# Folding the values of batches 1 to 3 head by head from 64 rows, in a gated attention and feed-forward kernel with a new prologue order

## The reference, cut to what matters

```python
q = layernorm(x) @ Wq; k = ctx @ Wk; v = ctx @ Wv          # per head
o = softmax(q @ k.T / 8) @ v                               # 77 keys
x = x + tanh(g_xattn) * (o @ Wo + bo)
n = layernorm(x)
g = act_quant(n) @ weight_quant(w_gate).T                  # 512 -> 2048
u = act_quant(n) @ weight_quant(w_up).T
h = square(relu(g)) * u
x = x + tanh(g_ffn) * (act_quant(h) @ weight_quant(w_down).T)
```

## Time and profile before

| | us |
|---|---|
| median of 3 runs | 1192.84 |
| the profiled execution, its own time | 1192.0 |
| its span | 1190.1 |
| PE busy | 1169.0 |
| DVE busy | 1035.5 |
| ACT busy | 869.1 |
| POOL busy | 307.0 |

### The profile page before, as it was taken

How to read it: one execution, slowest core, us unless ns; L and a number is a source line. 1 busy time by engine, 2 the same in 40 slices (tenths; PEclk the granted TensorE clock), 3 DMA queues, 4 the chain that set the end, 5 groups by cost and what they waited for, 6 DMA issues and landing times.

```text
span 1190.1 us, 18790 instructions
## 1 busy us (share of the span) xinstructions
PE 1169.0 (98%) x5802; PEld 742.8 (62%) x5867; DVE 1035.5 (87%) x2124; ACT 869.1 (73%) x929; POOL 307.0 (26%) x313
## 2 busy tenths in 40 slices
PE   9989899999999999999999999999999999999998
PEld 7656556666665666666566656656665666666554
DVE  4989898888988888888998888888899888988887
ACT  4877777776886777677877767776787777677764
POOL 3222222222442222222442222222244222222200
PEclk9999999999999999999999999999999999999999
DMA  9792654443444464444444464443443444444333
GB/s 354 263 302 67 156 142 109 98 108 93 101 115 102 114 167 110 97 103 107 101 99 98 114 178 112 98 107 94 101 114 97 104 97 110 96 99 112 84 65 75
DMA packets 286484, 144.69 MB, mean 122 GB/s; under 512 B 254586, under 2 KB 255226, under 8 KB 283889
## 3 DMA queue, kind: packets, MB, share of 16 engines
q1 hardware_dynamic: 286445, 144.32, 47.4%
q10 hardware_dynamic: 4, 0.00, 0.0%
HBM read 57.86 MB, written 24.35 MB: 69 GB/s over the span
## 4 chain that ended last, share of the span: by engine, by line
PE 88%; DVE 4%; DMA 3%; ACT 3%; issue 2%; SPq 0%; POOL 0%; ACTq 0%; DVEq 0%; POOLq 0%
PE gu_ps L1084 34%; PE o_ps L1048 18%; PE y_ps L1098 17%; PE s_ps L66 17%; DMA v_scr<-x 1%; DMA w_down<-in_wu_t 1%; DVE staged L1324 1%; PE gu_ps L1148 1%; DVE half_max L1330 1%; DMA a_scr<-a_spare 1%; DVE w_down L1484 0%; ACT staged L730 0%; ACT x L762 0%; PE y_ps L1141 0%; ACT k_pairs L864 0%
## 5 line engine op out<-in xcount | busy, mean ns | idle before, releaser
L1084 PE MATMUL gu_ps<-w_up,xq_t 128*128 128x512 bf16 x1024 | 241.9, 379 | 0.7 <-DVE staged L1324 0.7
L1084 PE MATMUL gu_ps<-w_gate,xq_t 128*128 128x512 bf16 x951 | 226.3, 379 | 8.6 <-DMA xq_t<-xq 3.9
L1098 PE MATMUL y_ps<-w_down,hq_t 128*128 128x512 bf16 x1008 | 227.8, 379 | 0.0
L1048 PE MATMUL o_ps<-v_sb,pt_high 128*128 128x512 f32 (+1 forms) x640 | 212.8, 413 | 1.1 <-DVE pt_low L1313 1.1
L1324 DVE TENSOR_TENSOR staged<-staged,gu_ps 128x1024 f32<-128x1024 f32 x128 | 155.6, 1215 | 53.8 <-ACT staged L784 53.8
L66 PE MATMUL s_ps<-a_sb,xf_high 128*128 128x308 f32 x1024 | 187.3, 305 | 0.0
L1084 PEld LDWEIGHTS gu_ps<-w_up,xq_t 128*128 128x128 bf16 x1024 | 99.5, 98 | 122.8 <-DVE staged L1324 2.6
L645 POOL TENSOR_TENSOR rstd<-var_eps,neg_half 128x1 f32<-128x1 f32 x128 | 96.6, 755 | 307.9 <-DVE var_eps L1289 275.2
L824 ACT ACTIVATE staged<-staged,h_scale 128x1024 f32<-128x1024 f32 x126 | 137.9, 1141 | 48.7 <-DVE h_scale L1344 48.7
L1098 PEld LDWEIGHTS y_ps<-w_down,hq_t 128*128 128x128 bf16 x1008 | 97.8, 97 | 119.7
L778 ACT ACTIVATE staged<-gu_ps 128x1024 f32<-128x1024 f32 x127 | 128.9, 1015 | 53.9 <-PE gu_ps L1084 53.5
(11 more groups left out here) (146 smaller groups left out, 1439.7 us busy)
## 6 DMA issues: line engine op xcount, KB each, us to landing
xf_sb<-in_x_feat SPq DMA_DIRECT2D x64, 256.0 KB, 2.7
x_sb<-in_x_tok SPq DMA_DIRECT2D x64, 256.0 KB, 2.8
y<-staged SPq DMA_DIRECT2D x63, 256.0 KB, 2.0
staged<-in_wg_t SPq DMA_DIRECT2D x4, 1024.0 KB, 9.8
staged<-in_wd_t SPq DMA_DIRECT2D x4, 1024.0 KB, 7.5
folded<-a_scr SPq DMA_DIRECT2D x3, 1232.0 KB, 5.3
v_scr<-x SPq DMA_DIRECT2D x12, 256.0 KB
folded<-v_scr SPq DMA_DIRECT2D x3, 1024.0 KB, 5.0
```

The source lines that it names most:

```text
L1048: last = nc.tensor.matmul(o_ps[:, :], pt[0:rows, P * c:P * (c + 1)], v_sb[0:rows, v, c, :], start=(c == 0 and pt is pt_high and v == 0), s ...
L1084: last = nc.tensor.matmul(target[:, q, :], xq_t[:, s.par(0), c, :], w[:, c, cols], start=(c == 0), stop=(c == DC - 1))
L1098: last = nc.tensor.matmul(y_ps[:, :], hq_t[:, c, :], w_down[:, c, :], start=(c == 0), stop=(c == FC - 1))
```

## The change

- Batch 0 keeps the fold by pairs of heads. For batches 1 to 3 the values of one head lie side by side (231 keys), and are folded in two halves of 116 and 115 keys by one matmul each that contracts the 64 rows of that head, taken right out of `v_t` at row 0 or row 64 (`tile_position`). That makes 16 matmuls with 16 copies (`take_later_values(k)`) in place of 24 matmuls with 15 copies. `place_values` stays for batch 0 alone.
- Each half lies over two batches, so it is stored by two DMAs, 32 in place of 15. The DRAM scratch is row by row, and `load_values` reads it in rows of 2 KB where it read 8 KB for each partition.
- Piece 0 of w_down is loaded into `v_pairs`, once the fold of batch 0 has read it, and no longer waits for a slot of `staged`. The first `relu_half` waits for the up piece in slot 0 and no longer for down piece 0.
- The prologue lists of all engines are new. SP issues all eight pieces of gate and up without a wait among them, ahead of the first key store; x of tile 0 comes ahead of the others, x_feat of tile 1 and x of tiles 1 to 3 behind the first key store, x_feat of tile 3 nearly last. DVE measures 5 pieces (4 before) and scales 6 (7 before); ACT measures 7 (8 before) and scales 6 counting the two of the first step (5 before).
- In the first step DVE's `top_half(0)` stands behind `shift_scores(3)`. The second step has a list of its own: `hidden_half(1)` right behind `unmark_input`, `probs_low` of the third tile within it, `sum_probs` last.

```diff
+FIRST_ROWS = ((BATCH - 1) * KEYS + 1) // 2
+V_LATER = 2 * HEADS
...
+def head_part(k):
+    h, s = divmod(k, 2)
+    return h, KEYS + FIRST_ROWS * s, FIRST_ROWS - s
...
         def raw(m, p):
+            if m == 2 and p == 0:
+                return v_pairs[:, :, :].rearrange("p q n -> p (q n)")[:, 0:PIECE]
...
                 def load_down(p):
-                    sp.wait_ge(weight_stage[1][UP_SLOT.index(p)], DONE)
+                    if p == 0:
+                        sp.wait_ge(vo_done, KC)
+                    else:
+                        sp.wait_ge(weight_stage[1][UP_SLOT.index(p)], DONE)
...
+                def store_later_values(k):
+                    at = KEYS * head_part(k)[0]
+                    sp.wait_ge(vo_taken, k + 1)
+                    for b, j, n, r in part_runs(k):
+                        sp.dma_start(v_scr[b, at + j:at + j + n, :],
+                                     v_slots[k % V_OUT_RING][r:r + n, :]).then_inc(v_stored[k % V_OUT_RING], 16)
...
+                def take_later_values(k):
+                    rows = head_part(k)[2]
+                    act.wait_ge(vo_done, KC + k + 1)
+                    if k >= V_OUT_RING:
+                        act.wait_ge(v_stored[k % V_OUT_RING], 32 * (k // V_OUT_RING))
...
+                def fold_later_values(k):
+                    h, first, rows = head_part(k)
+                    if k < V_RING:
+                        pe.wait_ge(v_split_done, KC + k - V_RING + 1)
+                    else:
+                        pe.wait_ge(vo_taken, k - V_RING + 1)
+                    own = slice(HEAD * (h % 2), HEAD * (h % 2 + 1))
+                    nc.tensor.matmul(value_slots[(KC + k) % V_RING][0:rows, :], v_t[own, h // 2, first:first + rows], wo_sb[own, h // 2, :],
+                                     start=True, stop=True, tile_position=(HEAD * (h % 2), 0)).then_inc(vo_done, 1)
...
# SP, the loads ahead of the first key store (after)
+                load_x(start, 0)
                 load_weight(1, 2, wu_t)
+                load_weight(0, 1, wg_t)
+                load_weight(1, 3, wu_t)
+                load_weight(0, 2, wg_t)
+                load_weight(0, 3, wg_t)
+                load_weight(1, 0, wu_t)
+                load_weight(1, 1, wu_t)
+                store_keys(1, 0)
...
# DVE, from the first measured piece of the new list (after)
+                measure(1, 3)
+                first_values_low(0)
+                measure(0, 2)
+                first_values_low(1)
+                top_scores(start, 0)
+                shift_scores(start, 0)
+                sum_rows(0)
+                measure(1, 0)
+                find_unit(0)
+                scale(0, 0)
+                sum_probs(start, 0)
...
+                scale(2, 0)
+                sum_probs(start, 2)
+                scale(2, 1)
+                ternary(2, 1, w_down)
+                probs_low(start, 1)
+                ternary(2, 0, w_down)
...
+                def second_step(s):
+                    unmark_hidden(s, -1)
+                    hidden_half(s, 0)
+                    add_attention(s, 1)
+                    input_scale(s, 1)
+                    top_scores(s, 3)
+                    unmark_input(s, 1)
+                    hidden_half(s, 1)
+                    shift_scores(s, 3)
+                    input_stats(s, 3)
+                    top_half(s, 0)
+                    probs_low(s, 2)
+                    hidden_unit_scale(s, 1)
+                    top_half(s, 1)
+                    hidden_scales(s)
+                    sum_probs(s, 3)
```

More of the change, by code:

```diff
@@ L955, in _ @@
                 gate_bias()
-                high_part(start, 1)
                 first_keys(2)
@@ L968, in _ @@
+                take_later_values(0)
+                scale(0, 2)
                 take_keys(1, 2)
-                first_values(3)
-                measure(1, 3)
+                take_later_values(1)
+                high_part(start, 1)
                 take_keys(1, 3)
-                first_values(4)
+                take_later_values(2)
+                take_later_values(3)
+                take_keys(2, 0)
+                take_later_values(4)
                 probs_high(start, 0)
-                take_keys(2, 0)
@@ new lines, in _ @@
+                take_later_values(7)
+                mark_input(start, 0)
+                measure(2, 1)
+                take_later_values(8)
+                exponentials(start, 1)
+                take_later_values(9)
+                take_keys(3, 0)
+                take_later_values(10)
+                measure(2, 3)
+                part_probs(start, 1)
+                take_keys(3, 1)
+                take_later_values(11)
+                take_later_values(12)
+                take_keys(3, 2)
@@ L1533, in first_step @@
                     hidden_half(s, 0)
-                    top_half(s, 0)
                     add_attention(s, 1)
@@ L1552, in step @@
                         return
-                    if s.has(1) and not s.opens(1) and s.has(3):
+                    if s.opens(1):
+                        second_step(s)
+                        return
+                    if s.has(1) and not s.opens(2) and s.has(3):
                         probs_low(s, 1)
@@ L1559, in step @@
                         finish(s, -2)
-                    if s.has(3) and not s.opens(1):
+                    if s.has(3):
                         input_stats(s, 3)
@@ L1621, in _ @@
-                split_bias()
-                dve.wait_ge(tanh_done, 1)
-                first_values_low(0)
-                measure(0, 3)
-                first_values_low(1)
-                sum_probs(start, 0)
-                sum_rows(0)
-                first_values_low(2)
+                ternary(0, 0, w_gate)
+                sum_rows(1)
+                scale(0, 1)
+                ternary(0, 2, w_gate)
+                ternary(0, 1, w_gate)
+                find_unit(1)
+                find_hidden_unit()
@@ L1629, in _ @@
+                probs_low(start, 0)
+                scale(1, 2)
+                scale(1, 0)
+                ternary(1, 3, w_up)
+                ternary(1, 0, w_up)
+                add_attention(start, 0)
+                input_scale(start, 0)
+                ternary(1, 1, w_up)
+                top_scores(start, 1)
+                shift_scores(start, 1)
+                unmark_input(start, 0)
+                ternary(1, 2, w_up)
+                sum_probs(start, 1)
                 dve.wait_ge(rstd1_done, 2)
@@ L1645, in _ @@
[L1645 to L1656 removed]
+                measure(2, 2)
                 top_scores(start, 2)
@@ L1668, in _ @@
                 ternary(2, 0, w_down)
-                probs_low(start, 1)
-                ternary(2, 1, w_down)
                 steps(dve, step, (-2, -1, 0, 1, 2, 3, 4))
```

316 lines of the change are left out of this document (128 added, 188 removed).

## The result

The changed kernel takes **1201.98 us** (median of 4 runs, 1201.02 to 1202.95), the kernel before 1193.20 beside it (4 runs, 1191.83 to 1194.35): a ratio of 1.0078, 95% interval 1.0063 to 1.0093. It is about 9 us slower, where 1189.3 was forecast and 1184.3 to 1196.0 given as range. The profiled execution has a span of 1199.2 us.

The account below looks back on a forecast made before the run. Steady steps go at PE's pace, so the start of gate_up(3, 0), paced by DVE and ACT, decides. The walk gave -2.6 us with crowded durations, -4.6 with usual ones; taken -3.5: 1192.84 - 3.5 = 1189.3 us, range 1184.3 to 1196.0.

Parts of the forecast that it names:

- The value stores: Prologue, values of batches 1 to 3: a round trip is two issues (0.9 us), a landing (4.25 to 6.94) and a copy (0.6).
- The slower rival: Prologue: value slots' round trips make the last take late, at 92.5 us, giving 1198 us; chance 0.18.
- the ring of three value slots: Value parts share three slots: five round trips where four sufficed, 8.0 us left for each; from about 9.2 the sign turns.
- PE's work: Prologue folds: eight fewer at 0.86 us each are 6.9 us less, lying beside DVE's work.
- the bound below: PE's folds: if neighbours in different row halves ran together, 4 x 0.86 = 3.4 us less.
- the prediction's bound above: PE's folds: 0.19 us for each of 16 if its weight load is no longer covered, 3 us more.
- Loads: Prologue: pieces land from 24.4 to 38.5 us; DVE's first measure starts 1.3 us later, row sums no longer wait 2.3 us.
- DVE's list: Prologue: 58.8 us of work from 27.2, waits under 0.3 us, first step at 86.0, 4.5 us ahead.
- ACT's end of the prologue: Join at 79.7 us against 82.31, relu at 85.5 against 88.13; gate_up(0, 0) starts at 82, not 85.42.
- the walk of the first step: ACT from relu to the mark of tile 1: 8.1 us, mark at 93.6 against 97.57, so -4.0 us.
- Second step: 3.4 us of PE waits removed, but later sum_probs delays the mark 2.7 us; some 2.4 us come back at tile 3.
- The reload in 2 KB rows: Reload of values lies beside the step's other work: nothing counted; if it showed, three reloads below 1 us each.

Follow-up runs that it names:

- e17: Changed kernel with x_feat of tile 3 loaded early, old second step, DVE's first_values_low(2) early and parts of 109 and 122 rows: 1190.31 us, ratio 0.9994.
- e16: Kernel before with each value store cut in two, 38 and 90 rows (52 and 52 of the last chunk): 1197.23 us, ratio 1.0037.
- e15: Kernel before with each value store cut in two, 64 and 64 rows (52 and 52 of the last chunk): 1192.12 us, ratio 0.9995.
- e4: Kernel before with the folds by heads alone (16 parts, 32 stores, 2 KB reload), prologue order and first two steps as before: 1198.34 us, ratio 1.0046.
- e14: Kernel before with the folds by heads alone, parts cut at 109 and 122 rows instead of 116 and 115: 1193.50 us, ratio 1.0016.
- e13: Changed kernel with the parts of a head cut at 109 and 122 rows instead of 116 and 115: 1198.83 us, ratio 1.0057.
- e9: Kernel before with the folds by heads alone, one store a part (18 stores instead of 32), rows in another order: 1206.63 us, ratio 1.0119.
- e18: Kernel before with the folds by heads alone, 18 stores, 112 rows a part, some rows left out: 1194.38 us, ratio 1.0023.
- e11: Kernel before with one fold matmul for each value chunk of batches 1 to 3 (15 in place of 24): 1193.40 us, ratio 1.0012.
- e5: Changed kernel with small unused matmuls (14, 7, 5 and 14) added at four places where PE waited: 1201.99 us, ratio 1.0058.
- e7: Changed kernel with x_feat of tile 3 early, DVE's old second step and small unused matmuls (14, 8, 4, 9) in PE's waits: 1196.53 us, ratio 1.0027.
- e2: Changed kernel with DVE's second step in the order of before: 1197.87 us, ratio 1.0040.
- e3: Changed kernel with x_feat of tile 3 loaded early and DVE's second step in the order of before: 1197.08 us, ratio 1.0036.
- e1: Changed kernel with x_feat of tile 3 loaded right behind the last down piece: 1200.97 us, ratio 1.0059.
- e8: Kernel before with the folds by heads alone, every odd part folded twice (24 matmuls, as many as before): 1200.25 us, ratio 1.0068.
- e6: Kernel before with the folds by heads alone, small unused matmuls added ahead of part 8 (16) and gate_up(1, 0) (14): 1198.74 us, ratio 1.0065.

## Why the prediction was wrong, point by point

The forecast was -3.5 us and the result is +9. Two terms have runs that size them in the changed kernel: the second step (+1 of gain forecast, 4 us of loss measured) and the value stores (nothing forecast beyond their round trip, about 3 us measured, with intervals that overlap). The late x_feat adds 1. With x_feat early, the old second step, no 38-row stores and DVE's low part early (e17) the time is level with before or below it.

**The value stores** (the step that failed first). The prediction priced a part's store as "two issues (0.9 us), a landing (4.25 to 6.94 us) and a copy", and let the down pieces land in the time of before. It never asked what 77, 39 and 38 rows do where 128 and 104 stood. What the runs showed: with the number of stores and the bytes the same, the rows of a store alone change the time, and 38 rows are bad. In the kernel before this costs 5.1 us (e16 over e15), in the head folds 4.8 (e4 over e14; intervals just overlap), in the changed kernel 3.1 (over e13; they overlap), and 116 and 115 rows cost 12.3 (e9 over e18). The Trainium skill states the rule ("DMA: Bandwidth & Descriptors", Why a DMA increments its semaphore by 16 and not by 1): a transfer that SP or ACT issues runs on the largest number of engines up to 16 that divides its outermost dimension, the lowest-numbered ones. By that rule 38 rows run on 2 engines, 116 on 4, 115 on 5, 112, 64 and 128 on 16. An estimate worked out from this rule, rows of 2 KB on the fullest engine over all value stores, stands in the table. The times of the kernels with pair folds (before, e15, e16) rise with it, and so do those with head folds, but for e18 and e14, whose intervals overlap. So the times agree with the rule; no view here shows single engines, so that these are the ones the page names is not shown.

| kernel | rows of its stores | rows on the fullest engine, by the page | us |
|---|---|---|---|
| e18 | 112, 56 | 117 | 1194.4 |
| before | 128, 104 | 120 | 1192.4 to 1192.9 |
| e15 | 64, 52 | 120 | 1192.1 |
| e14 | 77, 32, 45 | 152 | 1193.5 |
| e4 | 77, 39, 38 | 288 | 1198.3 |
| e16 | 38, 90, 52 | 324 | 1197.2 |
| e9 | 116, 115 (77, 39, 38 in two parts) | 400 | 1206.6 |

**The slower rival** (1198 us, chance 0.18) got the sign and the queue right and 5 of the 9 us, and the mechanism wrong: what it got right is luck. It was to be the ring of three value slots, with ACT waiting for value stores after 60 us. In the changed kernel no such wait shows; ACT waits for down pieces, key stores and x_feat. Waits of ACT for value stores show in other kernels with rows of 38, 115 or 116: 0.9 us in e4, 2.4 in e16, 2.9 in e9.

**PE's work.** Two halves. "It costs nothing at the end" was right for the work: 9 matmuls fewer gave nothing (e11). It left out the clock. In before it was at 1.00; in the changed kernel's trace, behind PE's wait from 36.5 to 39.96 us, it falls (the third number from the end):

```profile
40.00:44.00 4.00, 4.00 (x9) 1.87 (x10) 3.84 (x6) 3.38 (x5) 0.59 (x1) 0.68 0.68 228
44.00:48.00 4.00, 4.00 (x14) 2.15 (x12) 3.96 (x6) 1.88 (x2) 1.77 (x1) 0.50 0.64 251
```

What that is worth at the end of the changed kernel wasn't separated: e5 took this drop away, and another came at 80 us. Between executions of e5 and of e7 a lower clock went with some 7 us.

The price of 0.86 us for a 64-row fold was low for one that stands alone; the bound below held for neighbours in different halves:

```profile
49.35 1.11 PE L1239 MATMUL gu_ps<-folded,v_t 64*115 64x512 f32 x2
...
54.15 1.12 PE L1239 MATMUL gu_ps<-folded,v_t 64*115 64x512 f32 x4
```

Two records are one matmul: 1.11 us printed for one, and 1.12 for two; from start to start it is 1.05 us for either, against 0.86 of a 128-row one. The difference of 0.19 us is the prediction's bound above. Its working of that figure is off (3 x 0.86 leave 0.16 us to 2.74, not 0.19), but weight loads of the folds take 0.19 us in both traces, so the size fits; that it is the load, no longer covered, isn't shown. Eight matmuls fewer are 16 records fewer, as the trace has it (48 where before has 64); the 24 of the prediction is a slip. None of it reached the end.

**Loads.** Right: up piece 3 landed at 27.0 (forecast 27.2), gate piece 3 at 32.0 (32.9), with a wait of 1.5 us (2.2).

**DVE's list.** Forecast to end at 86.0, ended at 89.70, before at 90.55. Its waits between 28 and 85 us were 1.57, 0.86, 1.33 and 1.16 us where under 0.3 was forecast, two behind ACT and two behind PE; a ternary pass took 2.12 us where 1.47 was the slow one of the earlier trace rows. Even in e17 PE's first step starts at 84.39, not at the 82 of the forecast.

**ACT's end of the prologue.** "Join at 79.7, relu at 85.5" came out as 82.12 and 93.47. `part_probs(1)` ended at 77.56 where 73.9 was forecast: its input was ready at 73.53, but in ACT's list it stands behind the measuring of the down piece that took 7.5 us to land. `high_part(3)` then waited 4.41 us for x_feat. Both transfers lie on the queue of the first point. From relu on, the walk of the first step held: the mark of tile 1 begins 8.1 us behind it, as forecast, and its lateness is relu's.

**Second step.** The waits were foreseen and mis-sized. xq_t of tile 2 was no longer waited for, ACT's `part_probs(4)` waited 6.71 us for POOL, and PE for xq_t of tile 3, all as told. But the sum let 2.4 us of the 3.4 come back, a gain of 1. Measured, the new order costs 4 us against the old one (e2 below the changed kernel, e3 below e1). The traces agree: from `gate_up(1, 0)` to `gate_up(2, 0)` the changed kernel is 1.2 us quicker than e2, and from there to `gate_up(4, 0)` it takes 41.6 us where e2 and the kernel before take 36.3. POOL and DVE of the changed kernel in order of time:

```profile
126.70 1.13 POOL L669 TENSOR_TENSOR rstd<-var_eps,neg_half 128x1 f32<-128x1 f32 x1
```

```profile
127.87 0.22 DVE L1415 TENSOR_SCALAR x_top_n<-x_top,rstd 128x1 f32<-128x1 f32 x1 [0.44 <-POOL rstd L669]
...
130.70 0.78 DVE L1337 TENSOR_REDUCE prob_sum<-probs 128x8 f32<-128x616 f32 x1
```

`sum_probs(4)` starts at 130.70, 14.6 us behind the attention of tile 2, where 12.9 was forecast and 9.2 stood before. It waits for nothing there: DVE comes to it so late. On the way DVE waited 0.58 us for the mark, 0.52 for the square and 0.44 for a root of POOL, which stood behind `input_stats(4)`'s root in POOL's list, and `probs_low` took 1.51 us in place of 0.82. (`exponentials(4)` waited 1.40 us for that first root too, but was done 4 us before DVE asked for it.) Normalise, `part_probs(4)` and the mark follow, released 18.1 us behind the attention and not 16.2. Then come three terms that the sum did not have. PE waits 2.60 us for `relu_half(2, 0)`, which stands behind that mark. The clock is at the lower level behind this wait: eight gate matmuls at 137.36 take 3.38 us in place of 1.90. And the waits of 0.20 and 1.09 us that were to go came back one step later:

```profile
151.92 0.73 PE L1069 MATMUL o_ps<-v_sb,pt_high 128*128 128x512 f32 x2 [1.09 <-DVE pt_low L1344]
```

**The rest.** The reload in 2 KB rows opened no wait: from 166 us steps are 17.28 us apart as before. I had expected that, and it holds.

## What to carry to other kernels

When a change alters the shape of a DMA, price the shape and not only bytes and count. By the rule of the Trainium skill cited above, ask how the outermost row count divides over 16 engines, and keep it at a multiple of 16, or at least with a large divisor. Do so also for stores that nobody waits for: here loads of 1 MB beside them landed after 12.1 us in place of 8.0. A median landing that grows for a transfer that was not edited is the sign to look for, and a cut moved by a few rows is the cheap test. When a list is reordered, follow the moved instruction through every engine behind it and to the next steps: the second step's new order was to take away 3.4 us of waits and cost 4 on balance. And slack won on an engine that is not the bound was worth nothing here; gathered in one wait, it stood ahead of stretches at half clock, whose price at the end stays open.

## What the runs showed of the hardware that was not expected

- A store of 115 or 116 rows of 2 KB held back 1 MB loads issued near it to 12.1 us of landing, where 112 rows gave 8.0; one store in place of two made it worse (1206.6 against 1198.3 us).
- Fifteen more stores on SP's queue cost nothing (1192.12 against 1192.71 us).
- One program (e17) took 1188.3 us at a mean granted clock of 0.997 and 1197.3 at 0.990. The kernel before stood at 0.996 or more in all executions on record; every kernel with head folds had executions at 0.994 or below, those with a single PE wait of over 3.3 us in the profile's first 110 us (e4) as well as those with none over 2.8 (e8) or 2.1 us (e7). How long PE waited before a drop was not the same each time: the clock fell behind 1.57 us in the changed kernel (at 70.52, granted clock 0.66 from 70.5 to 75.5 us), and stood at 1.00 behind 2.07 us in the kernel before (at 120.95).
- Small matmuls in PE's waits raised the clock of e6's executions from 0.988 to 0.993 up to 0.994 to 0.997 and left the time as it was (1198.7 against 1198.3 us).
- Two neighbouring 64-row matmuls in different halves of the array took as long as one (1.05 us from start to start); one alone took longer than a 128-row one of the same 512 columns (1.05 against 0.86).
